# Mixer A: another order of TensorE's steps and of VectorE's convolutions within a super-tile

## The chip, the cores and the metric

The kernel is one program on one core of a Trainium2 chip. The metric is the device time of one execution in microseconds (us), the median of several runs. Everything is fp32. TensorE does matrix products into PSUM, ScalarE and VectorE take results out of PSUM and work on them, GpSimd works on SBUF alone, and SyncE issues the DMAs.

## The reference, cut to what matters

Four layers follow each other on x of shape (4, 1024, 512): mixer A, a feed-forward block, mixer B, the feed-forward block again. Each adds its result to x. The change is in mixer A, a state-space layer with 16 heads of 64 channels and a state of 64 per head:

```python
proj = x @ in_proj_w.T                       # gate z (1024), hBC (1152), dt (16)
conv = sum(xp[:, k:k + s, :] * conv_w[:, k] for k in range(4)) + conv_b
h, Bm, Cm = split(silu(conv));  dt = softplus(dt + dt_bias);  A_d = -exp(A_log) * dt
# in chunks: A_cs = cumsum(A_d); L = exp(segment_sum(A_d))
Y_diag = (C B^T * L) @ (h * dt)              # within a chunk
states = (B * decay)^T @ (h * dt)            # carried from chunk to chunk
Y_off  = (C @ state) * exp(A_cs)             # from the state before
yf = (Y_diag + Y_off + D * h) * silu(z)
out = (norm_w * yf * rsqrt(mean(yf * yf) + eps)) @ out_proj_w.T
```

## The kernel before, in words

**Tiling.** The 4096 tokens are cut into 16 super-tiles of 256, each of two tiles of 128 tokens (tile one is j=0, tile two is j=1). `mixer_phase` (L303) is used for both mixers; what differs comes from the head count. In mixer A `NS` is 2 and `NP` is 1 (two slots of eight heads in a tile), `NB` is 9 convolution blocks of 128 channels, and `FOLD` holds (the state lies in 128 partitions). In mixer B `NP` is 4, and the branches `if NP > 1` are its own; the change leaves their order as it is.

**Pipelining.** In super-tile i the kernel computes the scan, gate, norm and output of i, and in between the projections and convolutions of the next super-tile n = i+1. Fifteen of the sixteen super-tiles have such a next one.

**Order.** No planner is at work. `schedule` (L453) writes TensorE's steps by hand, and the blocks of ScalarE, VectorE and GpSimd write theirs; each engine runs its list strictly in order and waits on semaphores. In mixer A before the change a super-tile's TensorE steps are: head (`zza`, four transposes `xT`, `BG`, `zzb`, `prs`, `yoff0a/b`, `seg0.0`, `prt`, `xnT0`, `pout`, `xnT1`, `ident0`, `small1`), then `dt`, `blk0` to `blk8`, `state0`, `ydiag0.0`, `ydiag0.1`, `z0a`, `z0b`, `rs0`, `yoff1a/b`, `seg1.0`, `rt0`, `out0`, `z1`, `sums`, `z2`, `small0`, `state1`, `ident1`, `ydiag1.0`, `ydiag1.1`.

**Two banks.** All steps but `seg`, `ydiag`, `ident` and `xT` put their result in one of two PSUM banks in turn (`use`, L677). Each of them first waits until the result of the step before the last that used these banks has been taken out: `freed(pe, sec.uses[idx - 2], i, n)`. Which wait that is depends on the step (`freed`, L556): for a convolution block it is ScalarE's second copy (L891 copies the block, L892 scales it by the last tap), for a z step ScalarE's copy (L898), for `small` VectorE's two operations (L1266, L1267), for `sums` VectorE's copy (L1247), for `out0` VectorE's addition to the residual (`out_add`, L1352).

**TensorE lines in the rows.** L667 a block or z projection (8 matmul instructions a block of 128 channels), L691 `xnT`, L696 `dt`, L728 `small`, L747 `state`, L814 `ydiag`, L827 `ident`, L716 `sums`, L768 `out`, L737 `yoff`, L793 `seg`. Where a row says 128*64, an instruction uses 64 of the array's columns.

**VectorE.** `conv_blocks` (L1180) takes a group of one or two blocks through three taps, one scalar_tensor_tensor each (L1186), whose two tensor inputs `shared_pre` and `shared_cv` both lie in SBUF. `make_xdt` (L1240, in mixer B L1235) also has both inputs in SBUF. `small_sums` is L1266 and L1267; `exponent_sides` L1276 to L1281 makes the operands of `seg`; `from_state` L1296 takes `yoff` out; `slot_mult` L1307 multiplies a slot's 128x1024 decays by a mask, both inputs in SBUF; `out_scale` L92 to L94 and `out_add` L1352 follow the two slots of a tile; then come `halo`, `next_decays` and the next input's norm.

**ScalarE** takes the slots' exponents from `seg` (L948, L955), squares for the norm (L965) and copies.

**GpSimd.** As soon as `from_state` has written `y1` of a tile, three operations follow each other there: L1570 adds the skip path to `y1`, L1581 makes `xw`, L1587 decays the state. All three read SBUF.

Of the kernel before, what the change touches and what calls it, by code (L numbers as in the profile page):

```python
# [302 lines left out]
def mixer_phase(nc, sig, before, cfg, c, arena, later, psum, x_src, x_dst, w):  # L303
# [7 lines left out]
    H, HP, N, NS = cfg.H, cfg.HP, cfg.N, cfg.slots  # L311
# [13 lines left out]
    with ctx:  # L325
# [117 lines left out]
        def state_steps(j):  # L443
            return [f"state{j}"] if FOLD else [f"state{j}a", f"state{j}b"]

        def head(prev, nxt):
            return (["zza", "xT0", "xT1", "xT2", "xT3"] + b_and_g + ["zzb"]
                    + (["prs"] if prev else []) + ["yoff0a", "yoff0b", "seg0.0"] + (["prt"] if prev else [])
                    + (["xnT0"] if nxt else []) + (["pout"] if prev else [])
                    + (["seg0.1"] if NP > 1 else []) + (["xnT1"] if nxt else [])  # L450
                    + ["ident0", "small1"])

        def schedule(prev, nxt):  # L453

            steps = head(prev, nxt)
            if NP > 1:
                def diagonal(j, half):
                    return [f"ydiag{j}.{s}" for s in range(half * (NS // 2), (half + 1) * (NS // 2))]

                def when(names):  # L460
                    return names if nxt else []

                steps += when(["dt"] + blocks[0:2]) + diagonal(0, 0)
                steps += ["seg0.2"] + when(blocks[2:4]) + ["seg0.3"] + when(blocks[4:NB])
                steps += state_steps(0) + diagonal(0, 1) + when(["z0a", "z0b"])
                steps += ["rs0", "yoff1a", "yoff1b", "seg1.0", "rt0", "out0"]
                steps += ["seg1.1", "ident1"] + when(["z1"]) + diagonal(1, 0)
                steps += ["seg1.2"] + state_steps(1) + when(["sums"]) + ["seg1.3"]
                steps += when(["z2", "small0"]) + diagonal(1, 1)
                return steps  # L470
            for p in range(NP):
                steps += fill0[2 * p] if nxt else []
                steps += [f"seg0.{p + 1}"] if p + 1 < NP else []
                steps += fill0[2 * p + 1] if nxt else []
                if p + 1 == NP:
                    steps += state_steps(0)
                steps += [f"ydiag0.{2 * p}", f"ydiag0.{2 * p + 1}"]
            steps += ["z0a", "z0b"] if nxt else []
            steps += ["rs0", "yoff1a", "yoff1b", "seg1.0", "rt0", "out0"]
            for p in range(NP):  # L480
                steps += fill1[2 * p] if nxt else []
                steps += [f"seg1.{p + 1}"] if p + 1 < NP else (["sums"] if nxt else [])
                steps += fill1[2 * p + 1] if nxt else []
                if p + 1 == NP:
                    steps += (["small0"] if nxt else []) + state_steps(1)
                if p == 0:
                    steps += ["ident1"]
                steps += [f"ydiag1.{2 * p}", f"ydiag1.{2 * p + 1}"]
            return steps

        def unit_bank(p, k):
# [103 lines left out]
        with nc.Block() as block:  # L595
# [541 lines left out]
            def _(dve):  # L1137
# [22 lines left out]
                def dt_raw(sec):  # L1160
                    dve.wait_ge(work_full, sec.full("dt"))
                    nc.vector.tensor_tensor(raw[:], sec.bank("dt")[:, 0:2 * H].rearrange("p (j h) -> p j h", j=2),
                                            dt_bias[:].unsqueeze(1).to_broadcast([P, 2, H]), ALU.add
                                            ).then_inc(raw_ready, 1)
                    dve.wait_ge(raw_ready, FREE + sec.n + 1)
                    nc.vector.scalar_tensor_tensor(out=sp_e[:], in0=raw[:], scalar=-1.0, in1=raw[:],
                                                   op0=ALU.mult, op1=ALU.min).then_inc(nabs_ready, 1)

                def dt_finish(sec):

                    dve.wait_ge(sp_ready, sec.n + 1)
                    link(nc.vector.scalar_tensor_tensor(out=dt[:], in0=raw[:], scalar=0.0, in1=sp_e[:],
                                                        op0=ALU.max, op1=ALU.add))
                    link(nc.vector.tensor_tensor(a_step[:], dt[:], a_low[:].unsqueeze(1).to_broadcast([P, 2, H]),
                                                 ALU.mult))
                    link(nc.vector.tensor_scalar(a_step[:], a_step[:], -1.0, FLOOR, ALU.mult, ALU.max))
                    link(nc.vector.tensor_tensor(a_step[:], a_step[:], a_high[:].unsqueeze(1).to_broadcast([P, 2, H]),
                                                 ALU.mult))
# [82 lines left out]
                def small_sums(sec, j):  # L1261

                    dve.wait_ge(work_full, sec.full(f"small{j}"))
                    sums_of = sec.bank(f"small{j}")[0:R, 0:NSET * P]
                    flat = [t[0:R].rearrange("p k l -> p (k l)") for t in (hi, parts)]
                    link(nc.vector.tensor_scalar(flat[0], sums_of, c["sign_row"][0:R], None, ALU.mult))  # L1266
                    nc.vector.scalar_tensor_tensor(out=flat[1], in0=sums_of, scalar=c["low_row"][0:R],  # L1267
                                                   in1=flat[0].bitcast(F32), op0=ALU.mult, op1=ALU.add
                                                   ).then_inc(hilo_ready, 1)
# [55 lines left out]
                def gate(sec, j, halves=(0, 1)):  # L1325
                    tile = 2 * sec.i + j
                    dve.wait_ge(zs_done, sec.i + 1)
                    dve.wait_ge(sq_done, FREE + 2 * tile)
                    for half in halves:
                        dve.wait_ge(ydiag_done, FREE + 2 + tile * NS + (half + 1) * (NS // 2))  # L1330
                        cols = slice(half * 4, half * 4 + 4)
                        nc.vector.tensor_tensor(yz[:, cols, :],
                                                ybank[:, half * 512:(half + 1) * 512].rearrange("p (b t) -> p b t", b=4),
                                                zs[:, cols, j * P:(j + 1) * P], ALU.mult).then_inc(yz_done, 1)
# [28 lines left out]
                def supertile(sec, prev, nxt):  # L1363
# [14 lines left out]
                        out_add(sec, "pout", i - 1, 1)  # L1378
                    if NP > 1 and sec.ln is not None:
                        norm_stats(sec.ln)  # L1380
                    small_sums(sec, 1)
                    if not prev:
                        norm_into_w_out()
                    if NP > 1:
# [48 lines left out]
                        if nxt:  # L1433
                            exponent_sides(2 * sec.n)
                        return
                    for p in range(NP):
                        for g in (2 * p, 2 * p + 1):
                            if nxt and "dt" in fill0[g]:
                                dt_raw(sec)
                                dt_finish(sec)  # L1440
                            blks = [int(name[3:]) for name in fill0[g] if name != "dt"] if nxt else []
                            if g + 1 == NS and NP > 1:
                                state_add(sec, 0)
                                gate(sec, 0)
                            for k in range(0, len(blks), 2):
                                conv_blocks(sec, blks[k:k + 2])
                            if g % 2 == 0 and p + 1 < NP:
                                slot_mult(sec, 0, 2 * p + 2)
                                slot_mult(sec, 0, 2 * p + 3)
                            elif g % 2 == 0:  # L1450
                                exponent_sides(2 * i + 1)
                    if NP == 1:
                        state_add(sec, 0)
                        gate(sec, 0)
                    square_sums(sec, "rs0")
                    from_state(sec, 1)
                    rms_var(sec, "rt0")
                    slot_mult(sec, 1, 0)
                    slot_mult(sec, 1, 1)
                    out_scale(2 * i)  # L1460
                    out_add(sec, "out0", i, 0)
                    if nxt:
                        halo(sec)
                        next_decays(sec)
                        keep_column(sec)
                    for p in range(NP):
                        if p + 1 < NP:
                            slot_mult(sec, 1, 2 * p + 2)
                            slot_mult(sec, 1, 2 * p + 3)
                        if p == 0 and sec.ln is not None:  # L1470
                            norm_stats(sec.ln)
                        if p == min(1, NP - 1) and sec.ln is not None:
                            norm_apply(sec.ln)
                    if nxt:
                        sums(sec)
                        small_sums(sec, 0)
# [777 lines left out]
```

## Time and profile before

| | us |
|---|---|
| median of 3 runs (2848.24 to 2852.04) | 2849.39 |
| the profiled execution, its own time | 2849.16 |
| its span, first to last instruction | 2847.5 |
| TensorE matmul busy (share of the span) | 2717.1 (95%) |
| VectorE busy | 1962.7 (69%) |
| ScalarE busy | 1526.3 (54%) |
| GpSimd busy | 914.8 (32%) |
| super-tiles of mixer A | 65.8 or 67.5 each |

"Busy" of TensorE is modelled from pipelined matmuls, so consecutive rows of it overlap; the distance between the starts of two rows is what a step takes. A row of a timeline gives start, duration, engine, line, operation, output and inputs, shape and count, and in brackets the engine's idle time before it and who ended that.

### The profile page before, as it was taken

How to read it: one execution, taken by the hardware profiler on the slowest of the kernel's cores; microseconds unless marked ns; L12 is line 12 of the kernel's file. 1: busy time of each engine (PE TensorE's matmuls, PEld its weight loads, DVE VectorE, ACT ScalarE, POOL GpSimd, SP SyncE). 2: the span in 40 equal slices, each digit the busy share in tenths (PEclk: the TensorE clock that was granted, in tenths of full speed). 3: DMA queues.
4: the chain of work that ended last, by engine and by line, in shares of the span. 5: the costliest groups of instructions: out<-in, count | busy, mean ns of one | idle time of the engine just before them, and what ended most of it. 6: DMA issues, size and time to landing. Idle time of an engine off the chain costs nothing. (4 is left out here: it accounts for less than half of the span.)

```text
span 2847.5 us, 49834 instructions
## 1 busy us (share of the span) xinstructions
PE 2717.1 (95%) x17464; PEld 1857.9 (65%) x17464; DVE 1962.7 (69%) x3695; ACT 1526.3 (54%) x2418; POOL 914.8 (32%) x614
## 2 busy tenths in 40 slices
PE   7999999999999999996899999999999999997996
PEld 6777776676776665455766666776666776664454
DVE  5666666666666663377787788788788888784267
ACT  3444444444445442341577677766677777664242
POOL 2222223322222331243233443333443343332134
PEclk9999999999999999997999999999999999998998
DMA  4000000001000034145000000000000000031233
GB/s 126 23 23 22 22 22 22 22 27 32 22 22 22 15 114 149 57 148 205 12 23 23 22 22 15 22 22 22 22 14 15 22 22 22 15 119 74 105 119 133
DMA packets 79935, 139.59 MB, mean 49 GB/s; under 512 B 17896, under 2 KB 17896, under 8 KB 78832
## 3 DMA queue, kind: packets, MB, share of 16 engines
q1 hardware_dynamic: 70752, 125.92, 12.7%
q10 hardware_dynamic: 9104, 12.63, 1.3%
q8 instruction: 48, 0.79, 0.1%
q14 instruction: 31, 0.25, 0.0%
HBM read 104.98 MB, written 33.55 MB: 49 GB/s over the span
## 5 line engine op out<-in xcount | busy, mean ns | idle before, releaser
L667 PE MATMUL work<-b_xnT,shared_w 128*128 128x256 f32 x2304 | 531.0, 385 | 3.1 <-DVE b_parts L1267 1.6
L667 PE MATMUL work<-a_xnT,shared_w 128*128 128x256 f32 x2176 | 508.2, 391 | 1.3
L667 PEld LDWEIGHTS work<-b_xnT,shared_w 128*128 128x128 f32 x2304 | 429.5, 191 | 77.9 <-issue 17.0
L667 PEld LDWEIGHTS work<-a_xnT,shared_w 128*128 128x128 f32 x2176 | 418.1, 195 | 73.4 <-issue 12.3
L1307 DVE TENSOR_TENSOR b_decay<-b_decay,b_gt 128x1024 f32<-128x1024 f32 x256 | 347.1, 1383 | 80.7 <-ACT b_decay L955 80.2
L948 ACT ACTIVATE b_decay<-seg 128x1024 f32<-128x1024 f32 x256 | 252.2, 1026 | 198.8 <-PE seg L793 198.6
L1535 POOL TENSOR_TENSOR b_rhs<-b_l_side,of_head 128x1024 fp32r<-128x1024 f32 x32 | 97.9, 3058 | 595.4 <-DVE b_l_side L1276 595.4
L955 ACT ACTIVATE b_decay<-b_decay 128x1024 f32<-128x1024 f32 x256 | 263.9, 1068 | 0.0
L1570 POOL TENSOR_TENSOR a_y<-a_y,a_skip 128x1024 f32<-128x1024 f32 x32 | 90.9, 2840 | 484.1 <-DVE a_y L1296 484.1
L1186 DVE SCALAR_TENSOR_TENSOR shared_cv<-shared_pre,a_conv_w,shared_cv 128x256 f32<-128x256 f32 x432 | 189.7, 482 | 73.3 <-ACT shared_cv L892 67.6
L1186 DVE SCALAR_TENSOR_TENSOR shared_cv<-shared_pre,b_conv_w,shared_cv 128x256 f32<-128x256 f32 x480 | 214.9, 481 | 23.4 <-ACT shared_cv L892 16.1
L768 PE MATMUL work<-a_w_out,a_yz 128*128 128x512 f32 x512 | 228.6, 599 | 2.4 <-DVE a_y L1296 0.9
L768 PE MATMUL work<-b_w_out,b_yz 128*128 128x512 f32 x512 | 229.2, 601 | 0.5
L898 ACT COPY shared_z<-work 128x256 f32<-128x256 f32 (+1 forms) x192 | 84.9, 442 | 261.6 <-PE work L667 261.4
L891 ACT COPY shared_pre<-work 128x256 f32<-128x256 f32 x304 | 115.4, 380 | 177.9 <-PE work L667 177.9
L1307 DVE TENSOR_TENSOR a_decay<-a_decay,a_gt 128x1024 f32<-128x1024 f32 x64 | 136.5, 2153 | 84.9 <-ACT a_decay L955 84.4
L768 PEld LDWEIGHTS work<-a_w_out,a_yz 128*128 128x128 f32 x512 | 95.4, 191 | 112.0 <-issue 108.3
L768 PEld LDWEIGHTS work<-b_w_out,b_yz 128*128 128x128 f32 x512 | 95.7, 192 | 110.6 <-issue 108.6
L807 PE MATMUL y<-b_decay,b_xdt 128*32 128x128 f32 x4096 | 133.4, 279 | 12.0 <-DVE b_decay L1307 11.8
L807 PEld LDWEIGHTS y<-b_decay,b_xdt 128*32 128x32 f32 x4096 | 108.2, 111 | 44.7 <-DVE b_decay L1307 23.8
L1570 POOL TENSOR_TENSOR b_y<-b_y,b_skip 128x1024 f32<-128x1024 f32 x32 | 82.8, 2589 | 156.7 <-DVE b_y L1296 156.7
L1782 PE MATMUL y<-f_x1T,shared_pre 128*128 128x512 f32 x256 | 122.9, 610 | 0.0
(314 smaller groups left out, 4570.7 us busy)
## 6 DMA issues: line engine op xcount, KB each, us to landing
shared_x<-in_L_attn_a_x SPq DMA_DIRECT2D x16, 512.0 KB, 3.5
a_x_res<-in_L_attn_a_x SPq DMA_DIRECT2D x32, 256.0 KB, 2.6
x_mid<-a_x_res SPq DMA_DIRECT2D x32, 256.0 KB, 2.0
shared_w<-in_L_ffn_d_w SPq DMA_DIRECT2D x2, 4096.0 KB, 14.2
f_d_w<-in_L_ffn_d_w SPq DMA_DIRECT2D x2, 4096.0 KB, 14.7
f_x_res<-x_mid SPq DMA_DIRECT2D x8, 1024.0 KB, 5.8
f_bc_w<-x_mid SPq DMA_DIRECT2D x8, 1024.0 KB, 5.6
shared_x<-x_mid SPq DMA_DIRECT2D x16, 512.0 KB, 4.0
```

The costliest lines, as they stand in the source:

```text
L667: mm = nc.tensor.matmul(dst, w_in[:, k, col:col + m], xnT[:, k, :], start=(k == 0), stop=(k == KD - 1))
L768: mm = nc.tensor.matmul(bank[:, :], yz[:, k, :], w_out[:, k, :], start=(k == 0), stop=(k == KE - 1))
L807: mm = nc.tensor.matmul(ybank[32 * q:32 * q + 32, slot * P:(slot + 1) * P], xdt[:, j, 4 * slot + q, 16 * odd:16 * odd + 32], decay[:, slot ...
L891: nc.scalar.copy(pre[0:m, b, HALO:], bank[0:m, 0:SUP])
L898: nc.scalar.copy(z_raw[:, got[0]:got[-1] + 1, :], sec.bank(name)[:, 0:len(got) * SUP].rearrange("p (b t) -> p b t", t=SUP)).then_inc(z_rea ...
L948: nc.scalar.activation(decay[:, slot_buffer(j, s)].rearrange("p h l -> p (h l)"), seg[s % 2][:, :], ACT.Relu, scale=-1.0).then_inc(seg_tak ...
L955: nc.scalar.activation(d, d, ACT.Exp, scale=-1.0).then_inc(exp_done, 1)
L1186: ins = nc.vector.scalar_tensor_tensor(out=cv[0:m, b, :], in0=pre[0:m, b, t:t + SUP], scalar=conv_w[0:m, b, t:t + 1], in1=cv[0:m, b, :], o ...
L1307: nc.vector.tensor_tensor(d, d, gt[:, j].unsqueeze(1).to_broadcast([P, 8, P]), ALU.mult).then_inc(m_ready, 1)
L1535: nc.gpsimd.tensor_tensor(rhs[1][:], l_side[:, 1].unsqueeze(1).to_broadcast([P, 8, P]), c["of_head"][:].unsqueeze(2).to_broadcast([P, 8, P ...
L1570: nc.gpsimd.tensor_tensor(y1[:], y1[:], skip[:], ALU.add).then_inc(y1x_ready, 1)
L1782: mm = nc.tensor.matmul(ybank[:, (m % 2) * 512:(m % 2 + 1) * 512], gate_w[:, k, m * P:(m + 1) * P], x1T[n][:, k, :], start=(k == 0), stop= ...
```

## The change

In `schedule`, for mixer A, `small1` moves from before `dt` to between `blk8` and `state0`; `z2` moves ahead of `sums`; `ident1` moves from behind `state1` to ahead of `small0`. So `small`, `state` and the two `ydiag` stand side by side in both tiles. On VectorE only six blocks are convolved ahead of `small_sums(1)`; `exponent_sides` of tile two comes after tile one's `gate`; blocks 6 and 7, then 8, are convolved after `from_state(1)` and `rms_var`, ahead of the two `slot_mult` of tile two. The new list in mixer A reads:

`... xnT1, ident0, dt, blk0 to blk8, small1, state0, ydiag0.0, ydiag0.1, z0a, z0b, rs0, yoff1a/b, seg1.0, rt0, out0, z1, z2, sums, ident1, small0, state1, ydiag1.0, ydiag1.1`.

```diff
--- before.py
+++ after.py
@@ -448,7 +448,7 @@
                     + (["prs"] if prev else []) + ["yoff0a", "yoff0b", "seg0.0"] + (["prt"] if prev else [])
                     + (["xnT0"] if nxt else []) + (["pout"] if prev else [])
                     + (["seg0.1"] if NP > 1 else []) + (["xnT1"] if nxt else [])
-                    + ["ident0", "small1"])
+                    + ["ident0"] + (["small1"] if NP > 1 else []))
 
         def schedule(prev, nxt):
 
@@ -473,19 +473,12 @@
                 steps += [f"seg0.{p + 1}"] if p + 1 < NP else []
                 steps += fill0[2 * p + 1] if nxt else []
                 if p + 1 == NP:
-                    steps += state_steps(0)
+                    steps += ["small1"] + state_steps(0)
                 steps += [f"ydiag0.{2 * p}", f"ydiag0.{2 * p + 1}"]
             steps += ["z0a", "z0b"] if nxt else []
             steps += ["rs0", "yoff1a", "yoff1b", "seg1.0", "rt0", "out0"]
-            for p in range(NP):
-                steps += fill1[2 * p] if nxt else []
-                steps += [f"seg1.{p + 1}"] if p + 1 < NP else (["sums"] if nxt else [])
-                steps += fill1[2 * p + 1] if nxt else []
-                if p + 1 == NP:
-                    steps += (["small0"] if nxt else []) + state_steps(1)
-                if p == 0:
-                    steps += ["ident1"]
-                steps += [f"ydiag1.{2 * p}", f"ydiag1.{2 * p + 1}"]
+            steps += ["z1", "z2", "sums"] if nxt else []
+            steps += ["ident1"] + (["small0"] if nxt else []) + state_steps(1) + ["ydiag1.0", "ydiag1.1"]
             return steps
 
         def unit_bank(p, k):
@@ -1378,7 +1371,8 @@
                         out_add(sec, "pout", i - 1, 1)
                     if NP > 1 and sec.ln is not None:
                         norm_stats(sec.ln)
-                    small_sums(sec, 1)
+                    if NP > 1:
+                        small_sums(sec, 1)
                     if not prev:
                         norm_into_w_out()
                     if NP > 1:
@@ -1433,28 +1427,21 @@
                         if nxt:
                             exponent_sides(2 * sec.n)
                         return
-                    for p in range(NP):
-                        for g in (2 * p, 2 * p + 1):
-                            if nxt and "dt" in fill0[g]:
-                                dt_raw(sec)
-                                dt_finish(sec)
-                            blks = [int(name[3:]) for name in fill0[g] if name != "dt"] if nxt else []
-                            if g + 1 == NS and NP > 1:
-                                state_add(sec, 0)
-                                gate(sec, 0)
-                            for k in range(0, len(blks), 2):
-                                conv_blocks(sec, blks[k:k + 2])
-                            if g % 2 == 0 and p + 1 < NP:
-                                slot_mult(sec, 0, 2 * p + 2)
-                                slot_mult(sec, 0, 2 * p + 3)
-                            elif g % 2 == 0:
-                                exponent_sides(2 * i + 1)
-                    if NP == 1:
-                        state_add(sec, 0)
-                        gate(sec, 0)
+                    if nxt:
+                        dt_raw(sec)
+                        dt_finish(sec)
+                        for k in (0, 2, 4):
+                            conv_blocks(sec, (k, k + 1))
+                    small_sums(sec, 1)
+                    state_add(sec, 0)
+                    gate(sec, 0)
+                    exponent_sides(2 * i + 1)
                     square_sums(sec, "rs0")
                     from_state(sec, 1)
                     rms_var(sec, "rt0")
+                    if nxt:
+                        conv_blocks(sec, (6, 7))
+                        conv_blocks(sec, (8,))
                     slot_mult(sec, 1, 0)
                     slot_mult(sec, 1, 1)
                     out_scale(2 * i)
@@ -1463,14 +1450,9 @@
                         halo(sec)
                         next_decays(sec)
                         keep_column(sec)
-                    for p in range(NP):
-                        if p + 1 < NP:
-                            slot_mult(sec, 1, 2 * p + 2)
-                            slot_mult(sec, 1, 2 * p + 3)
-                        if p == 0 and sec.ln is not None:
-                            norm_stats(sec.ln)
-                        if p == min(1, NP - 1) and sec.ln is not None:
-                            norm_apply(sec.ln)
+                    if sec.ln is not None:
+                        norm_stats(sec.ln)
+                        norm_apply(sec.ln)
                     if nxt:
                         sums(sec)
                         small_sums(sec, 0)
```

## Rows read from the trace of the kernel before

**Rows 1.** Windows of single super-tiles: PE, PEld, DVE, ACT, POOL busy, clock, DMA.

```profile
384.69:450.48 65.79, 64.86 (x372) 46.59 (x371) 42.09 (x87) 31.77 (x57) 19.33 (x12) 1.00 0.07 24
450.48:517.96 67.48, 66.55 (x372) 47.78 (x371) 42.12 (x87) 31.77 (x56) 19.34 (x12) 0.97 0.07 23
```

**Rows 2.** Timeline of TensorE in the super-tile from 384.69.

```profile
398.65 1.04 PE L827 MATMUL y<-ident,a_y 128*128 128x128 f32 x8
399.84 0.44 PE L728 MATMUL work<-tri_le,a_aa 128*64 128x128 f32 x4 [0.15 <-DVE a_x_res L1352]
400.21 1.96 PE L696 MATMUL work<-shared_w,a_xnT 128*128 128x16 f32 x16
402.01 15.79 PE L667 MATMUL work<-a_xnT,shared_w 128*128 128x256 f32 x72
417.73 1.08 PE L747 MATMUL work<-a_xw,a_bt 128*64 128x512 f32 x4
418.64 1.92 PE L814 MATMUL y<-a_decay,a_xdt 128*64 128x128 f32 x32
420.49 3.72 PE L667 MATMUL work<-a_xnT,shared_w 128*128 128x256 f32 x16
...
437.64 0.30 PE L716 MATMUL work<-a_aa,tri_le 128*128 128x32 f32 x2
...
438.00 0.39 PE L716 MATMUL work<-a_aa,ones 128*128 128x32 f32 x2
438.48 3.72 PE L667 MATMUL work<-a_xnT,shared_w 128*128 128x256 f32 x16
442.13 0.44 PE L728 MATMUL work<-tri_le,a_aa 128*64 128x128 f32 x4
442.88 1.08 PE L747 MATMUL work<-a_xw,a_bt 128*64 128x512 f32 x4 [0.31 <-ACT shared_z L898]
443.88 1.09 PE L827 MATMUL y<-ident,a_y 128*128 128x128 f32 x8
444.91 1.97 PE L814 MATMUL y<-a_decay,a_xdt 128*64 128x128 f32 x32
446.81 1.99 PE L667 MATMUL work<-a_xnT,shared_w 128*128 128x256 f32 x8
```

**Rows 3.** Timeline of ScalarE in it.

```profile
418.11 0.57 ACT L892 ACTIVATE shared_cv<-work,a_conv_b,a_conv_w 128x256 f32<-128x256 f32 x1
```

**Rows 4.** Timeline of VectorE in it.

```profile
414.36 6.78 DVE L1186 SCALAR_TENSOR_TENSOR shared_cv<-shared_pre,a_conv_w,shared_cv 128x256 f32<-128x256 f32 x15
...
425.87 1.29 DVE L1296 TENSOR_TENSOR a_y<-work,a_e 128x512 f32<-128x512 f32 x2 [0.73 <-PE work L737]
...
429.70 4.90 DVE L1307 TENSOR_TENSOR a_decay<-a_decay,a_gt 128x1024 f32<-128x1024 f32 x2 [2.44 <-ACT a_decay L955]
...
435.45 0.75 DVE L1352 SCALAR_TENSOR_TENSOR a_x_res<-work,a_rr,a_x_res 128x512 f32<-128x512 f32 x1 [0.22 <-DVE a_rr L94]
```

**Rows 5.** Timeline of GpSimd in it.

```profile
427.32 2.36 POOL L1570 TENSOR_TENSOR a_y<-a_y,a_skip 128x1024 f32<-128x1024 f32 x1 [26.43 <-DVE a_y L1296]
429.63 1.91 POOL L1581 TENSOR_TENSOR a_xw<-a_xdt,a_e 128x1024 f32<-128x1024 f32 x1
431.62 1.90 POOL L1587 TENSOR_TENSOR a_state<-a_state,a_e_fold 128x512 f32<-128x512 f32 x1
```

**Rows 6.** Timelines in mixer B: VectorE, then GpSimd, then VectorE elsewhere.

```profile
1461.21 3.46 DVE L1235 TENSOR_TENSOR b_xdt<-b_xt,b_dt 128x512 f32<-128x512 f32 x2
...
1461.21 2.90 POOL L1570 TENSOR_TENSOR b_y<-b_y,b_skip 128x1024 f32<-128x1024 f32 x1 [3.65 <-DVE b_y L1296]
...
1567.42 2.35 DVE L1307 TENSOR_TENSOR b_decay<-b_decay,b_gt 128x1024 f32<-128x1024 f32 x2
```

**Rows 7.** Windows of TensorE where its clock changes: busy (instructions), clock, DMA.

```profile
464.00:468.00 4.00, 3.84 (x34) 1.00 0.17 66
468.00:471.00 3.00, 3.00 (x8) 0.50 0.31 87
```

## The prediction

> **What bounds the kernel now.** I read the page first: TensorE is busy 95% of the span, no other engine over 69%. A mean over four layers says little about one of them, so I cut mixer A by super-tile. One without a fall of the clock takes 65.79 us and TensorE is busy in 64.86 of it [rows 1]; VectorE has 23.7 us free in the same stretch. The reader should see two things there. First, removing TensorE's visible idle time can give at most 0.93 us a super-tile, so a gain must also come out of what the modelled busy time hides. Second, two kinds of super-tile exist, 65.79 and 67.48 us: seven of the fourteen that I cut so have the longer time and a mean granted clock of 0.97 instead of 1.00. The fall follows the thin stretch of `small1` and `dt`, sixteen-column matmuls: at 464 to 468 us the granted clock is 1.00, at 468 to 471 us it is 0.50, 1.2 instead of 2.4 GHz [rows 7]. A fall costs 67.48 - 65.79 = 1.69 us.
>
> Then I read the timelines of one super-tile, engine by engine [rows 2 to 5], measuring a TensorE step from start to start. VectorE and GpSimd are not the bound, but TensorE can be held by them through the two banks, so for each step that changes its place I asked which result it now waits for.
>
> **Tile one on TensorE.** `small1` goes from before `dt`: 400.21 - 399.84 = 0.37 us less there [rows 2]. The 0.15 us wait ahead of it is for the residual addition of `pout`, which `dt` now has to wait for itself, so it stays. `small1` comes back behind `blk8`. By instructions that costs 0.27 us, since the change of array shape (128 to 64 columns) is then paid once for both. But the step before the last is now `blk8`, not `blk7`, when `state0` starts. ScalarE finishes `blk8`'s second copy at 418.11 + 0.57 = 418.68 us [rows 3]. Everything here is 0.37 earlier, so 418.31, and with 0.05 for the semaphore `state0` starts at 418.36 instead of 417.73 [rows 2]: 0.63 us later. `small1` is hidden in that wait and costs nothing more. The same wait is seen today in tile two, 0.31 us ahead of L747 [rows 2]. Tile one: **+0.63 us**. Bounds: -0.1 if the copy were ready (then 0.27 of `small1` against 0.37), +0.7.
>
> `z0a` now waits for VectorE's `small_sums(1)`, which comes behind the convolutions of blocks 4 and 5. These end near 414 us, as today's fifteen-operation row from 414.36 shows that six operations take 2.7 [rows 4], and `z0a` starts after 420 [rows 2]: nothing. `gate` comes earlier, since three blocks fewer stand ahead of it; the 1.7 us of `exponent_sides` behind it lie beside ScalarE's squares and `rs0`: nothing, and at worst 0.3.
>
> **Tile two on TensorE.** From the start of `sums` to the next `zza` it is 446.81 - 437.64 = 9.17 us [rows 2]. In the new order: `z2` 16 instructions at 15.72 / 72 = 0.218, 3.49; `sums` 0.6 (two of six instructions begin at 438.00, the rest of the 0.84 is `z2` waiting for `z1`'s copy); `ident1` 1.03 less a change of shape, 0.9; the change to 64 columns, 0.1; `small0` 0.27; `state1` 0.91; the two `ydiag` and the change back 1.85, as in tile one [rows 2]. Sum 8.1, so **-1.1 us** (bounds -0.9 and -1.2). What goes is the wait of `z2` for `z1`, that of `state1` for `z2` (hidden behind `sums` and `ident1`) and two changes of shape, some 0.1 to 0.15 each. What is late next is ScalarE's chain from `sums` to the silus, since `sums` moves behind `z2`; it is gated today by `z2`'s copy anyway, and stays within 0.1 us of where it is.
>
> **The convolutions on VectorE.** This is the term that decides. Blocks 6, 7 and 8, nine operations at 6.78 / 15 = 0.45 = 4.07 us [rows 4], are put at 427.2 us, behind `from_state(1)` (425.87 + 1.29) and into the 2.44 us in which VectorE waits for the exponents [rows 4]. Taken alone they would delay the first `slot_mult` by 1.6 us. But exactly there GpSimd starts its three operations: 427.32, 429.63, 431.62 to 433.52 us [rows 5]. Today the convolutions run while GpSimd is idle, the 26.43 us ahead of L1570 [rows 5].
>
> What happens when both want SBUF shows at `slot_mult`. Free, two take 2.35 us in mixer B [rows 6], 1.18 each; here two take 4.90 [rows 4]. The second ends at 434.60, that is 1.08 us after GpSimd's last operation ends at 433.52 [rows 4, 5]: it ran only when GpSimd had done. The other direction: GpSimd's L1570 takes 2.36 us free and 2.90 us when it meets the first L1235 of mixer B, and the pair of L1235 ends at 1464.67, 0.56 us (one half-size operation) after that L1570 ends at 1464.11 [rows 5, 6]. So a VectorE operation with two SBUF inputs and a GpSimd operation exclude each other for their whole length. A convolution tap is such an operation. No row shows one against GpSimd, so its price has bounds: 0 and the whole of GpSimd's time.
>
> I take the whole. Nine taps are 4.07; GpSimd's three are 2.36 + 1.91 + 0.9 (its third lasts 1.90, of which it waits about 1.0 for the first `slot_mult`) = 5.17. GpSimd has an operation ready at all times there, so whichever goes first, the last tap ends at 427.2 + 4.07 + 5.17 = 436.44. Two free `slot_mult` follow, 2.35, and then as today 436.20 - 434.60 = 1.60 to the end of `out_add` [rows 4]: 440.4 us, 4.2 later than today.
>
> In the old order `sums` waits for that `out_add`; in the new one `z2` does, in the same place, at 437.64. Today there is 1.44 us to spare (437.64 - 436.20). With the delay TensorE stands for 440.45 - 437.64 = **2.8 us**, and some 0.1 more to start again (an estimate: the two changes of shape in the rows cost about that, and there too the next weights are not loaded ahead). Behind it TensorE waits with `z2`, `sums`, `ident1` and all that follows. The 0.63 us of tile one moves both sides alike. Behind the stop nothing else is late: `next_decays` and the norm follow `out_add` within about 4 us, and `sums` comes 3.5 us after `z2` starts.
>
> The Trainium skill, page "SBUF — State Buffer", section "Who interferes with whom", says that a VectorE instruction with two SBUF inputs contends with a GpSimd instruction that reads SBUF, and that the pair of ports is held for the whole instruction. By this rule the taps are caught as the other operations are, and the sum is the one above; without it the term would be zero. The trace agrees for L1307 and L1235; no row shows L1186 so.
>
> **The clock.** The thin stretch ahead of the blocks gets shorter by `small1`, so I expect most of the seven falls to go: -11.8 us. The stop of 2.8 us is a new thin place, thinner than that one, and `z2` behind it is dense. Bounds are no fall there and one in each of 15; I take six, +10.1 us.
>
> **Sum.** +0.63 - 1.1 + 2.8 + 0.1 = +2.4 us in each of the 15 super-tiles with a next one, 36 us; with the clock 36 - 11.8 + 10.1 = +34. The last super-tile (-0.2) and the other layers don't change. The profiled execution took 2849.16 us (span 2847.5 and 1.7 around it), 0.2 below the median, so no correction: 2849 + 34 = **2883 us**, 1.2% slower. Its own range is 2868 to 2902: no fall gives 2873, fifteen falls 2899.
>
> **The rivals.**
>
> (a) Faster: the taps don't meet GpSimd, or VectorE gets all its turns first. For it: no row shows a tap against GpSimd, and the 2.44 us gap is there. Against: L1307 and L1235, and GpSimd's third operation, which got in between two `slot_mult`. The last tap then ends at 427.2 + 4.07 = 431.3, the `slot_mult` at 434.7 at the latest, `out_add` at 436.3, inside the 1.44 us to spare. Then 15 x (0.63 - 1.1) = -7, and -11.8 to 0 of the clock: 2831 to 2842, say 2833. It decides from the point where the delay of `out_add` is under 1.44 us. Chance 0.13.
>
> (b) The stop is about half: VectorE and GpSimd share rather than exclude, so that taps take twice their time while GpSimd is at work. The last tap then ends near 434.5, `out_add` at 438.5, the stop is 0.9 to 1.4 us. 15 x (+0.4 to +0.9), and -11.8 with 3 us of new falls: 2846 to 2855. Chance 0.07; against it, that two `slot_mult` end with GpSimd plus one operation and not at twice their time.
>
> (c) As forecast, but the clock falls in nearly every stop: 2849 + 36 - 11.8 + 25 = 2898. For it: 3 us of nothing is less than `small1` and `dt`. Against: seven in fourteen today, so place in time matters too. Chance 0.14.
>
> (d) The forecast itself: 0.66.
>
> **Chances.** About 0.2% (5.7 us) is what a measurement of this kernel can tell from no change. Faster 0.13 is (a), same 0.07 is (b), slower 0.80 is (c) and (d). The range goes from 2852, where the upper part of (b) is taken in, to 2902.
>
> **What would show it.** Right: TensorE idle 2.5 to 3 us ahead of an L667, put down to VectorE's residual addition, once in each of 15 super-tiles; taps of 2 us or more beside GpSimd; 0.7 us idle ahead of the first `state`, put down to ScalarE's L892; no wait ahead of the second. Wrong: taps that stay at 0.48 us each while GpSimd is busy, and super-tiles under 65.8 us. The clock step is wrong if the number of falls in mixer A stays at seven ahead of the blocks.

## The result and the profile after

| | us |
|---|---|
| before, median of 4 runs (2848.24 to 2852.04) | 2850.25 |
| after, median of 4 runs (2869.66 to 2872.61) | 2871.47 |
| ratio of after to before | 1.0074 (95% interval 1.0061 to 1.0087) |
| span of the profiled execution, before and after | 2847.5, 2870.1 |

The change makes the kernel slower by 21 us. Windows of two super-tiles of mixer A in the changed kernel, columns as in [rows 1], the first with a fall of the clock (a stretch in which TensorE is granted 1.2 instead of 2.4 GHz) and the second without:

```profile
325.28:394.39 69.11, 66.13 (x371) 47.81 (x370) 44.36 (x87) 32.02 (x57) 18.96 (x12) 0.98 0.07 23
394.39:461.79 67.40, 64.43 (x371) 46.62 (x370) 44.31 (x87) 32.02 (x57) 18.93 (x12) 1.00 0.07 23
```

A super-tile without a fall takes 67.40 us instead of 65.79 [rows 1], and TensorE is busy 0.43 us less in it: what was added is idle time. From the first super-tile's start to the sixteenth's it is 1022.2 us instead of 999.1. Without the falls of the clock, seven before and six after at 1.69 us, that is 1.65 us more in each of 15, 24.8 in sum; one fall less gives 1.7 back. The 23.1 us that remain are nearly the whole difference of the spans (22.6); the rest of the kernel almost cancels. Its largest part is the sixteenth super-tile, 2.2 us shorter than before up to the first matmul of the feed-forward block (63.87 and 61.65 us, first row before, second after), at a mean granted clock of 0.97 instead of 0.95:

```profile
1050.96:1114.83 63.87, 56.06 (x341) 34.17 (x340) 32.57 (x63) 23.34 (x35) 20.83 (x15) 0.95 0.49 185
1075.01:1136.66 61.65, 54.44 (x342) 33.84 (x341) 32.77 (x63) 23.38 (x35) 20.86 (x15) 0.97 0.52 195
```

The timeline of TensorE in the super-tile from 394.39 of the changed kernel answers to [rows 2]:

```profile
427.06 0.44 PE L721 MATMUL work<-tri_le,a_aa 128*64 128x128 f32 x4
428.06 1.08 PE L740 MATMUL work<-a_xw,a_bt 128*64 128x512 f32 x4 [0.56 <-ACT shared_cv L885]
428.97 1.92 PE L807 MATMUL y<-a_decay,a_xdt 128*64 128x128 f32 x32
...
444.52 3.62 PE L660 MATMUL work<-a_xnT,shared_w 128*128 128x256 f32 x16
450.00 3.72 PE L660 MATMUL work<-a_xnT,shared_w 128*128 128x256 f32 x16 [1.87 <-DVE a_x_res L1345]
453.56 0.30 PE L709 MATMUL work<-a_aa,tri_le 128*128 128x32 f32 x2
...
454.15 1.07 PE L820 MATMUL y<-ident,a_y 128*128 128x128 f32 x8
455.15 0.44 PE L721 MATMUL work<-tri_le,a_aa 128*64 128x128 f32 x4
455.42 1.03 PE L740 MATMUL work<-a_xw,a_bt 128*64 128x512 f32 x4
456.27 1.92 PE L807 MATMUL y<-a_decay,a_xdt 128*64 128x128 f32 x32
458.12 1.99 PE L660 MATMUL work<-a_xnT,shared_w 128*128 128x256 f32 x8
```

Two waits stand out: 0.56 us ahead of `state0` (428.06) for ScalarE's second copy of `blk8`, and 1.87 us ahead of `z2` (450.00) for VectorE's residual addition. The wait ahead of `state1` is gone: `small0` starts at 455.15 and `state1` at 455.42.

VectorE beside it, which answers to [rows 4]. The third and fourth row are closer cuts into the nine taps of the second, and hold two taps each:

```profile
436.20 1.29 DVE L1289 TENSOR_TENSOR a_y<-work,a_e 128x512 f32<-128x512 f32 x2 [0.73 <-PE work L730]
...
437.53 8.56 DVE L1179 SCALAR_TENSOR_TENSOR shared_cv<-shared_pre,a_conv_w,shared_cv 128x256 f32<-128x256 f32 x9
446.01 2.35 DVE L1300 TENSOR_TENSOR a_decay<-a_decay,a_gt 128x1024 f32<-128x1024 f32 x2
...
449.20 0.75 DVE L1345 SCALAR_TENSOR_TENSOR a_x_res<-work,a_rr,a_x_res 128x512 f32<-128x512 f32 x1 [0.22 <-DVE a_rr L94]
...
437.53 2.98 DVE L1179 SCALAR_TENSOR_TENSOR shared_cv<-shared_pre,a_conv_w,shared_cv 128x256 f32<-128x256 f32 x2
...
437.93 4.62 DVE L1179 SCALAR_TENSOR_TENSOR shared_cv<-shared_pre,a_conv_w,shared_cv 128x256 f32<-128x256 f32 x2
```

GpSimd in the same place, against [rows 5]:

```profile
437.65 2.58 POOL L1552 TENSOR_TENSOR a_y<-a_y,a_skip 128x1024 f32<-128x1024 f32 x1 [27.07 <-DVE a_y L1289]
440.18 2.09 POOL L1563 TENSOR_TENSOR a_xw<-a_xdt,a_e 128x1024 f32<-128x1024 f32 x1
442.35 1.10 POOL L1569 TENSOR_TENSOR a_state<-a_state,a_e_fold 128x512 f32<-128x512 f32 x1
```

Nine taps of 0.45 us last from 437.53 to 446.09, 8.56 us. The second tap ends at 437.53 + 2.98 = 440.51, 0.28 us after GpSimd's L1552 ends at 440.23; the third at 437.93 + 4.62 = 442.55, 0.28 after L1563. GpSimd's first two are each 0.2 us longer than in [rows 5], where they waited for no tap (2.58 for 2.36, 2.09 for 1.91); its third takes 1.10 us here, against the 0.9 that the prediction estimated for it alone and that no run shows. The two `slot_mult` come behind GpSimd and take 2.35 us instead of 4.90, which gives back part of it.

### The profile page after: what moved, and what is told of

Its sections match the earlier page's. It is cut to its first block and busy times, and to the rows that moved or that the text cites. A ratio compares the mean times of both kernels' runs of the same rounds, so it can differ in the third digit from the quotient of the medians.

```text
span 2870.1 us, 49834 instructions
## 1 busy us (share of the span) xinstructions
PE 2706.8 (94%) x17464; PEld 1856.1 (65%) x17464; DVE 1998.9 (70%) x3695; ACT 1530.1 (53%) x2418; POOL 909.3 (32%) x614
## 5 line engine op out<-in xcount | busy, mean ns | idle before, releaser
L1179 DVE SCALAR_TENSOR_TENSOR shared_cv<-shared_pre,a_conv_w,shared_cv 128x256 f32<-128x256 f32 x432 | 257.1, 635 | 74.0 <-ACT shared_cv L885 68.3
L1552 POOL TENSOR_TENSOR a_y<-a_y,a_skip 128x1024 f32<-128x1024 f32 x32 | 94.5, 2952 | 480.9 <-DVE a_y L1289 480.9
L1300 DVE TENSOR_TENSOR a_decay<-a_decay,a_gt 128x1024 f32<-128x1024 f32 x64 | 98.9, 1567 | 48.5 <-ACT a_decay L948 48.0
L1552 POOL TENSOR_TENSOR b_y<-b_y,b_skip 128x1024 f32<-128x1024 f32 x32 | 82.9, 2590 | 156.6 <-DVE b_y L1289 156.6
```

Of the source, the lines that this page charges most:

```text
L1179: ins = nc.vector.scalar_tensor_tensor(out=cv[0:m, b, :], in0=pre[0:m, b, t:t + SUP], scalar=conv_w[0:m, b, t:t + 1], in1=cv[0:m, b, :], o ...
L1300: nc.vector.tensor_tensor(d, d, gt[:, j].unsqueeze(1).to_broadcast([P, 8, P]), ALU.mult).then_inc(m_ready, 1)
L1552: nc.gpsimd.tensor_tensor(y1[:], y1[:], skip[:], ALU.add).then_inc(y1x_ready, 1)
```

## The experiments

The first four share their runs of the kernel before (median 2851.2), the other three too (2850.59). "Super-tile" is the time of one without a fall of the clock, "falls" are those of the profiled execution in super-tiles 2 to 15 of mixer A; the longer stretch at the lower clock in the first super-tile, which every kernel has (10 to 14 us), is not counted.

| kernel | super-tile, us | falls | median, us | ratio to before (95%) |
|---|---|---|---|---|
| before | 65.79 | 7 | 2850 to 2851 | 1 |
| after | 67.41 | 6 | 2871.47 | 1.0074 (1.0061 to 1.0087) |
| e1_taps_early | 65.27 | 0 | 2826.69 | 0.9912 (0.9895 to 0.9928) |
| e2_taps_only | 68.22 | 14 | 2892.42 | 1.0122 (1.0079 to 1.0164) |
| e3_small_pool | 65.27 | 0 | 2827.26 | 0.9914 (0.9897 to 0.9930) |
| e4_tile1_only | 66.42 | 0 | 2846.47 | 0.9983 (0.9973 to 0.9992) |
| e5_state_first | 64.63 | 0 | 2815.48 | 0.9875 (0.9859 to 0.9892) |
| e6_block8_gap | 65.27 | 0 | 2826.18 | one run |
| e7_tile2_only | 64.64 | 2 | 2822.56 | 0.9900 (0.9883 to 0.9916) |

**e1_taps_early.** From the changed kernel, VectorE only:

```diff
-                        for k in (0, 2, 4):
+                        for k in (0, 2, 4, 6):
                             conv_blocks(sec, (k, k + 1))
...
                     exponent_sides(2 * i + 1)
+                    if nxt:
+                        conv_blocks(sec, (8,))
                     square_sums(sec, "rs0")
...
-                    if nxt:
-                        conv_blocks(sec, (6, 7))
-                        conv_blocks(sec, (8,))
                     slot_mult(sec, 1, 0)
```

> The changed kernel with blocks 6 and 7 convolved right behind 4 and 5, and block 8 behind exponent_sides, so that no tap runs beside GpSimd's three operations of tile two; TensorE's order is the changed one. Theory (the taps behind GpSimd hold out_add, and that holds z2): the wait of TensorE for out_add goes, 1.9 to 2.1 us a super-tile; a super-tile without a clock fall is 65.4 us (changed kernel 67.4, before 65.8), the total 2830 to 2842. Rival (the new TensorE order itself costs, through the wait ahead of state0 and through z2 waiting for out_add): the super-tile stays near 67.4 and the total near 2871.

Measured: super-tile 65.27, total 2826.7. The timelines of TensorE, then of VectorE, of this kernel:

```profile
412.57 0.44 PE L721 MATMUL work<-tri_le,a_aa 128*64 128x128 f32 x4
413.57 1.08 PE L740 MATMUL work<-a_xw,a_bt 128*64 128x512 f32 x4 [0.56 <-ACT shared_cv L885]
...
430.02 7.07 PE L660 MATMUL work<-a_xnT,shared_w 128*128 128x256 f32 x32
436.93 0.30 PE L709 MATMUL work<-a_aa,tri_le 128*128 128x32 f32 x2
...
418.70 1.52 DVE L1179 SCALAR_TENSOR_TENSOR shared_cv<-shared_pre,a_conv_w,shared_cv 128x256 f32<-128x256 f32 x3
...
425.54 4.90 DVE L1300 TENSOR_TENSOR a_decay<-a_decay,a_gt 128x1024 f32<-128x1024 f32 x2 [2.44 <-ACT a_decay L948]
...
431.28 0.75 DVE L1345 SCALAR_TENSOR_TENSOR a_x_res<-work,a_rr,a_x_res 128x512 f32<-128x512 f32 x1 [0.22 <-DVE a_rr L94]
```

`z1` and `z2` are one row of 32 instructions now, with no wait between them; out_add ends at 432.03, well ahead of `z2`'s place at 433.5. Where the nine taps stand is worth 67.41 - 65.27 = 2.14 us a super-tile, 32 us; the rival is out. The total came out 3 us under the range that I gave.

**e2_taps_only.** The kernel before, VectorE only; its blocks 6, 7 and 8 go where the change puts them:

```diff
+                            blks = [k for k in blks if k < 6]
                             for k in range(0, len(blks), 2):
                                 conv_blocks(sec, blks[k:k + 2])
...
                     rms_var(sec, "rt0")
+                    if nxt:
+                        conv_blocks(sec, (6, 7))
+                        conv_blocks(sec, (8,))
                     slot_mult(sec, 1, 0)
```

> The kernel before, with only the convolutions of blocks 6, 7 and 8 moved behind rms_var of tile two; TensorE's order is untouched. Theory: taps of 1.2 to 2.6 us beside GpSimd, and sums (which then waits for out_add) stops TensorE for about 2 us, of which 0.25 comes back since z2 no longer waits for z1's copy: super-tile 67.5 us without a fall, total 2873 to 2890. Rival (the order is what costs): 2850, within 0.2% of before.

TensorE, then VectorE, of this kernel:

```profile
444.74 3.62 PE L667 MATMUL work<-a_xnT,shared_w 128*128 128x256 f32 x16
450.80 0.41 PE L716 MATMUL work<-a_aa,tri_le 128*128 128x32 f32 x2 [2.44 <-DVE a_aa L1221]
...
437.76 8.57 DVE L1186 SCALAR_TENSOR_TENSOR shared_cv<-shared_pre,a_conv_w,shared_cv 128x256 f32<-128x256 f32 x9
...
449.44 0.75 DVE L1352 SCALAR_TENSOR_TENSOR a_x_res<-work,a_rr,a_x_res 128x512 f32<-128x512 f32 x1 [0.22 <-DVE a_rr L94]
...
450.56 0.19 DVE L1221 TENSOR_SCALAR a_aa<-a_a_step 128x64 f32<-128x64 f32 x1
```

The taps take the same 8.57 us, and now `sums` is what waits, 2.44 us. It stops 0.5 us longer than `z2` did, since it needs not the residual addition but `next_decays` behind it (L1221 ends at 450.75), which I had not counted: super-tile 68.22, not 67.5, and the total 2892.4, 2 over the range that I gave. The falls are told below. So the taps' place alone makes the kernel before slower, 68.22 - 65.79 = 2.43 us a super-tile.

**e3_small_pool.** The changed kernel, GpSimd only, in tile two (`j == 1`):

```diff
-                    nc.gpsimd.tensor_tensor(y1[:], y1[:], skip[:], ALU.add).then_inc(y1x_ready, 1)
+                    few = HP if j == 1 and not PADDED else E
+                    nc.gpsimd.tensor_tensor(y1[:, 0:few], y1[:, 0:few], skip[:, 0:few], ALU.add).then_inc(y1x_ready, 1)
```

and in the same way `xw` and the decay of the state.

> The changed kernel, but GpSimd's three operations of tile two (skip added to y1, xw, decay of the state) work on one head's 64 columns only; the other columns of the three are left out. Taps stay where the change put them. Theory (exclusion of the two engines): all nine taps take 0.48 us, out_add ends at most 1 us later than before, no stop ahead of z2: super-tile 65.4 us, total 2830 to 2842. Rival (the taps themselves are too much work for that place, whatever GpSimd does): a stop of 1 us or more stays, total over 2855.

VectorE, then GpSimd, of this kernel:

```profile
423.95 4.25 DVE L1179 SCALAR_TENSOR_TENSOR shared_cv<-shared_pre,a_conv_w,shared_cv 128x256 f32<-128x256 f32 x9
428.13 2.35 DVE L1300 TENSOR_TENSOR a_decay<-a_decay,a_gt 128x1024 f32<-128x1024 f32 x2
...
431.32 0.75 DVE L1345 SCALAR_TENSOR_TENSOR a_x_res<-work,a_rr,a_x_res 128x512 f32<-128x512 f32 x1 [0.22 <-DVE a_rr L94]
...
424.07 0.55 POOL L1553 TENSOR_TENSOR a_y<-a_y,a_skip 128x64 f32<-128x64 f32 x1 [27.06 <-DVE a_y L1289]
424.58 0.47 POOL L1565 TENSOR_TENSOR a_xw<-a_xdt,a_e 128x64 f32<-128x64 f32 x1
425.13 0.44 POOL L1572 TENSOR_TENSOR a_state<-a_state,a_e_fold 128x64 f32<-128x64 f32 x1
```

With the taps exactly where the change put them the nine take 4.25 us, and the super-tile is 65.27, that of e1_taps_early to 0.01. So the taps by themselves cost no stop there, and GpSimd's operations by themselves cost none either (e1_taps_early, where the two `slot_mult` meet them and take 4.90 us). The stop needs both, since their times add.

**e4_tile1_only.** As e1_taps_early, with TensorE's tile two as before:

```diff
-            steps += ["z1", "z2", "sums"] if nxt else []
-            steps += ["ident1"] + (["small0"] if nxt else []) + state_steps(1) + ["ydiag1.0", "ydiag1.1"]
+            steps += (["z1", "sums", "z2", "small0"] if nxt else []) + state_steps(1)
+            steps += ["ident1", "ydiag1.0", "ydiag1.1"]
```

> As the first of these, but TensorE's order of tile two as before (z1, sums, z2, small0, state1, ident1): what is left of the change is small1 between blk8 and state0. Theory: the wait of state0 for ScalarE's second copy of blk8 costs 0.6 us net: super-tile without a fall 66.4 us, +9 to +10 us; if the falls ahead of the blocks go with the shorter thin stretch, -11.8, so a total of 2846 to 2860; against the first kernel +1.0 to +1.1 us in each of 15 super-tiles, 16 us. Rival (grouping the 64-column steps is what pays in tile one too): below 2845.

Measured: 66.42 us, 0.63 over before, and no fall. Against e1_taps_early the order of tile two is worth 66.42 - 65.27 = 1.15 us. That the total is 4.7 us under before and not the 2.4 of this sum (9.4 - 11.8) may be the scatter of its runs (2842 to 2851). Its profiled execution bears the sum out where it applies, 997.3 us for the 15 super-tiles instead of 999.1, though the whole span is 2848.5 us, 1.0 over before's; the rest lies outside these super-tiles. One super-tile of this kernel, columns as in [rows 1]:

```profile
385.37:451.79 66.42, 64.93 (x371) 46.59 (x370) 42.26 (x87) 31.92 (x57) 19.35 (x12) 1.00 0.07 24
```

**e5_state_first.** As e1_taps_early, and:

```diff
-                    steps += ["small1"] + state_steps(0)
+                    steps += state_steps(0) + ["small1"]
...
-                    small_sums(sec, 1)
                     state_add(sec, 0)
+                    small_sums(sec, 1)
                     gate(sec, 0)
```

> The kernel with the taps early, and state0 ahead of small1 instead of behind it (VectorE's state_add and small_sums change places too). state0 then waits for blk7's copy, which is long done, and small1 for blk8's, which ends while state0 runs. Theory: the 0.56 us wait ahead of state0 goes and with it the second start of a 64-column step, 0.7 us a super-tile: 65.27 becomes 64.5 to 64.6, no falls of the clock among them, total 2815 to 2818. Rival (z0a, which now waits for VectorE's state_add, takes the place of the wait): 65.2, total 2826.

TensorE of this kernel:

```profile
393.79 15.79 PE L660 MATMUL work<-a_xnT,shared_w 128*128 128x256 f32 x72
409.51 1.08 PE L740 MATMUL work<-a_xw,a_bt 128*64 128x512 f32 x4
410.51 0.44 PE L721 MATMUL work<-tri_le,a_aa 128*64 128x128 f32 x4
410.78 1.92 PE L807 MATMUL y<-a_decay,a_xdt 128*64 128x128 f32 x32
412.62 3.72 PE L660 MATMUL work<-a_xnT,shared_w 128*128 128x256 f32 x16
```

`state0` follows the blocks without a wait, `small1` hides behind it, and the super-tile is 64.63. This is the fastest kernel of the study, 1.2% under before. Inside a super-tile it is no better than the old order of tile one: e7_tile2_only, below, has `small1` ahead of `dt` and takes 64.64. Most of what separates the two totals is the clock, two falls there and none here, and 3.1 us in the sixteenth super-tile.

**e6_block8_gap.** The changed kernel with blocks 6 and 7 early (`for k in (0, 2, 4, 6)`) and `conv_blocks(sec, (8,))` alone left ahead of the `slot_mult`.

> The changed kernel with blocks 6 and 7 convolved early and only block 8's three taps left beside GpSimd. Theory (VectorE pays for GpSimd's operations, not for the number of taps, but the two slot_mult pay for them anyway): the three taps take about 0.5, 2.6 and 2.0 us, the first slot_mult still meets GpSimd's third operation, out_add ends about 1.0 us later than without taps there, under the 1.44 us to spare: no stop ahead of z2, super-tile 65.3 us, total 2825 to 2830. Rival (each tap left there costs its share of the 2 us stop): 65.9 us, 2836.

VectorE of this kernel:

```profile
422.74 5.04 DVE L1179 SCALAR_TENSOR_TENSOR shared_cv<-shared_pre,a_conv_w,shared_cv 128x256 f32<-128x256 f32 x3
427.71 3.19 DVE L1300 TENSOR_TENSOR a_decay<-a_decay,a_gt 128x1024 f32<-128x1024 f32 x2
...
431.74 0.75 DVE L1345 SCALAR_TENSOR_TENSOR a_x_res<-work,a_rr,a_x_res 128x512 f32<-128x512 f32 x1 [0.22 <-DVE a_rr L94]
```

Three taps take 5.04 us and the two `slot_mult` 3.19, so out_add ends at 432.49, 0.5 us later than in e1_taps_early; since this super-tile starts 0.3 us earlier than that one (379.61 and 379.89), it is 0.75 us later within the super-tile. No stop, 65.27. Three taps or nine meet the same three operations of GpSimd. What the other six add is only their own 2.7 us (out_add ends 52.88 us into the super-tile here and 55.56 in the changed kernel), and that is what passes the 1.44 us to spare.

**e7_tile2_only.** The kernel before with the changed kernel's `steps` of tile two (the two lines with `-` in e4_tile1_only), nothing else.

> The kernel before with TensorE's new order of tile two alone (z1, z2, sums, ident1, small0, state1); small1 stays ahead of dt and VectorE's order is untouched. Theory: 1.1 to 1.2 us less in each super-tile, 64.6 without a fall; small1 and dt still stand together, so the falls of the clock behind them stay in a part of the super-tiles, 4 to 9 of 15: total 2829 to 2842. Rival for the clock (the falls left with something else, not with small1's place): none or one, total 2820 to 2826.

One super-tile without a fall:

```profile
378.24:442.87 64.63, 64.10 (x372) 46.72 (x371) 42.18 (x87) 31.86 (x56) 19.33 (x12) 1.00 0.08 24
```

Measured: 64.64, 1.15 us under before, as between e1 and e4. There are two falls, which is neither the 4 to 9 of the theory nor the none or one of the rival, and the total of 2822.6 lies in the rival's range. So tile two's order alone takes five of the seven falls away, while `small1` stays ahead of `dt`; moving `small1` alone takes all seven (e4_tile1_only). Both also change the length of a super-tile, so these counts, of one profiled execution each, don't separate the stretch of small matmuls from its place in time.

**Where the clock falls.** Windows of TensorE in e2_taps_only: busy (instructions), granted clock, DMA share and rate:

```profile
685.00:689.00 4.00, 3.84 (x34) 1.00 0.17 66
689.00:692.00 3.00, 3.00 (x8) 0.51 0.34 87
726.00:730.00 4.00, 1.57 (x11) 1.00 0.17 66
730.00:733.00 3.00, 3.00 (x9) 0.50 0.31 87
```

Both thin places are in this kernel, and behind each the clock is at half: at 689.0, 17.5 us into the super-tile, behind `small1` and `dt`, and at 730.0, 58.5 us into it, behind the stop ahead of `sums`, which ended at 728.7. In the kernel before all seven falls lie at the first place, in the changed kernel all six at 55.8 to 55.9 us, just behind the stop ahead of `z2`, which ends 55.6 us into the super-tile. The five experiments without the stop and with `small1` away from `dt` have none; e7_tile2_only, with `small1` there, has two, at 17.5.

## Why the prediction was right

The waits came where they were forecast, and the term that decides, the stop, came from the cause that was given; its size was too large, so the forecast of 2883 us stands 12 above the 2871 measured. Of the signs named for being right, the two waits, their releasers and the 15 stops were there, but the idle time was 1.87 us and not 2.5 to 3, and 0.56 and not 0.7.

- **Tile one, +0.63 us.** Measured +0.63, twice (e4_tile1_only against before, e1_taps_early against e7_tile2_only), with the wait ahead of `state0` where it was put.
- **Tile two, -1.1 us.** Measured -1.15, twice, with both orders of tile one.
- **Nothing for `z0a`, `gate`, `exponent_sides`, the silus.** No wait of TensorE for them is in the profile after. `small_sums(1)` ended at 428.29, 2.5 us before `z0a` started at 430.82. Blocks 4 and 5 did not end where the prediction put them, near 414: its row gives 414.36 + 2.7 = 417.1 for the kernel before, and in the kernel after they ended at 425.6, 31.2 us into the super-tile, which answers to 415.9. It made no difference.
- **The taps against GpSimd, 2.8 + 0.1 us.** Measured 2.14, and 15 x 0.76 us is the 11 or 12 by which the forecast is too high. This is the term that was mis-sized. TensorE was idle for 1.87 us instead of 2.8, and starting again cost about 0.26 instead of 0.1 (from `z1` to `sums` it is 9.04 us here and 6.91 in e1_taps_early). Most of the missing idle time is in the taps, which end after 8.56 us and not after 9.24. The exclusion for the whole length was read from 1024-element operations: a `slot_mult` ends 1.08 us after GpSimd's operation, of 1.22 that it lasts alone, so only 0.14 of it is covered. A tap ends 0.28 us after it, of 0.48, so 0.20 is covered, and three of the nine taps meet this. The Trainium skill, page "SBUF — State Buffer", section "SBUF: two separate sides", says that whichever of the two engines starts first gets the pair of ports for the whole instruction. The trace of the changed kernel agrees that the two take turns, but a tap lengthens GpSimd's operation by only about 0.2 us of its 0.48; whether the ports are free for the rest or the start of one instruction runs beside the end of the other, no run here shows.
- **The clock, 11.8 us back and 10.1 us new.** Six falls were forecast at the stop and six came; none is left behind `dt`. That the number was hit is luck: the same kind of stop in e2_taps_only has no fall in super-tiles 2 to 8 and one in each from 9 to 15. The reason given for the seven that went, the shorter stretch without `small1`, is borne out by e4_tile1_only, which has none with tile two as before; but it is not the only thing that counts, since five go in e7_tile2_only with that stretch unchanged.
- **The last super-tile, -0.2 us.** In the profiled executions it was 2.2 us shorter. No row gave the term, and the forecast had no clock in it; before, TensorE had the lower clock there for 6.8 us, after for 3.4.
- **Rival (a)** falls with e2 and e3; **rival (b)**, sharing, with the three taps that end 0.28 us after GpSimd's operations, whatever the length of these (2.58, 2.09 and 1.10 us), though in size the 1.87 us of idle time lie between its 0.9 to 1.4 and the 2.8 of the forecast; **rival (c)** with six falls in 15 stops, though e2_taps_only shows it can come so: from its ninth super-tile on the clock falls in each stop, and its runs lie from 2874 to 2900.

Without its taps the change is worth 15 x (0.63 - 1.15) = -7.8 and -11.8 for the falls, 19.6 us faster, close to the sum of rival (a). In e1_taps_early it is 18.9 us less from the start of the first super-tile to that of the sixteenth. The spans differ by 22.6 us; 3.9 of that is the sixteenth super-tile, 63.87 us in the kernel before (the row above) and 59.93 here, at the full clock:

```profile
1032.53:1092.46 59.93, 52.74 (x341) 33.26 (x340) 32.75 (x63) 23.36 (x35) 20.84 (x15) 1.00 0.54 203
```

The medians differ by 24.5 us, since the profiled execution of the kernel before, 2849.2 us, is 2 us faster than the median of the runs beside e1_taps_early.

## What to carry to other kernels

When work is moved into a gap of VectorE, look at what GpSimd does in that gap: in these traces each VectorE instruction with two SBUF inputs that met a GpSimd operation ended only after it, so three taps of 0.48 us took 5.04 us. Ask also who pays for GpSimd already: three taps there stopped nothing, since the `slot_mult` behind them paid less, while nine added 2.7 us of their own and passed the 1.44 us to spare. With two banks used in turn, an order of steps is an order of waits: after any swap, name for each step the result that now stands two before it, and who takes it out. And where a step must wait for a result, put another step's work into that wait, as `state0` covers `blk8`'s copy for `small1` in e5_state_first.

## What the runs showed that was not expected

- A tap of 256 elements holds GpSimd off for about 0.2 us and needs 0.28 us after GpSimd's end, of the 0.48 it lasts alone; a `slot_mult` of 1024 elements needs 1.08 of 1.22.
- The five experiments with 0.37 us less of small matmuls ahead of the blocks and no stop have no fall of the clock in super-tiles 2 to 15, against seven before (7 x 1.69 = 11.8 us, more than the 15 x 0.63 = 9.4 that the wait ahead of `state0` costs). Moving `small1` is enough for that (e4_tile1_only), but tile two's order alone also brought seven down to two.
- In e2_taps_only the falls start in the ninth super-tile and then come twice in each: super-tiles of 71.6 us instead of 68.2 with the same instructions.
